# Second attention's last step moved into the closing stage, and the opening's joined weights scaled before a tile's norm

## The chip, the cores and the metric

The kernel runs on one core of one Trainium2 chip. The metric is device time in microseconds (us) of one execution. The kernel before took 2147.05 us (median of three runs, 2145.66 to 2149.94).

## The reference

Two transformer layers with adaptive layer norm run one after the other on x of shape (2, 1024, 512). For each layer, six modulation vectors come from a small projection of a conditioning input:

```python
mod = (silu(c) @ wmod)                              # sa, ca, ga, sb, cb, gb
h = layernorm(x) * (1 + ca) + sa
x = x + ga * attention(h, ...)
h = layernorm(x) * (1 + cb) + sb
x = x + gb * ffn(h, ...)
```

Layer 0's attention has 32 heads with a latent key and value of width 32, RMS norms and rotary parts of width 64. Its feed-forward adds experts weighted by a sparsemax. Layer 1's attention has 32 heads of width 16 that share one key and one value:

```python
scores = einsum('bqhd,bkd->bhqk', q, k) * scale     # causal
probs = softmax(scores);  out = einsum('bhqk,bkd->bqhd', probs, v) @ wo
```

Its feed-forward is a product with a weight to which a masked, Fourier-transformed low-rank update is added ("w_feed1").

## The kernel before

The kernel is one sequence of stages, and each engine's order of work is written out by hand. Each stage is a block: within it every engine runs its own list, held together by semaphores, and at its end all engines meet before the next block begins. The stages are: constants; opening; attention of layer 0; middle (closing of layer 0, queries and keys of layer 1); attention of layer 1; closing. Between some blocks stands `clear` (L63), a block of its own in which the sync engine sets every semaphore of a group to zero, one instruction for each, while the other engines wait.

**The end of layer 1's attention** (`attention1`, L1578). Its work goes in 16 steps (`STEPS1`) of 4 heads, and every step has two halves of 512 query columns. The TensorE adds up four heads' values and sums of probabilities in the PSUM tile `op`, and ScalarE copies each half out into `u_sb` (`copy_out`, L1670). The sync queue then runs `results(t)` (L1615): four transfers move the heads' rows to `att_t`, one writes the sums to DRAM (L1620), and, when that has landed, one reads them back spread over 128 partitions as `den` (L1622). VectorE takes the reciprocal (L1723). The sync queue runs `reciprocals(t)` (L1624): one transfer writes them to DRAM (L1626), and four read them back, each row broadcast over 16 partitions, as `spread` (L1632). GpSimd multiplies the step's 64 rows of `att_t` by `spread` (L1698). For steps 0 to 14 this runs beside the next step's scores. For step 15 nothing else is left. After it come the end of the block, a `clear` of the stage's 26 semaphores (24 in `ATT1`, L1099, and the two `q_in`), and the closing block.

**The closing stage** (`closing`, L1865). It handles 16 tiles of 128 rows (`ALL`), of which the first 8 belong to the first batch entry. Step 15 writes rows of the second entry alone, which tile 8 is the first to read. For tile n: ScalarE rounds the attention output to `a_hi` (`outcome`, L1947), GpSimd forms the remainder `a_lo` (L1962), the TensorE multiplies both with the output weights in 12 matmuls (`project`: L1896, L1897, and L1900 for `a_lo`), VectorE gates it, adds the input tile `xt` and takes the norm's statistics (`first`, L1983 to L1991), ScalarE takes the root, VectorE normalises into `xn` (L1998), the TensorE transposes (L1907), ScalarE modulates and rounds (`modulate`, L1939, L1943), GpSimd forms the remainder `h_lo` (`normed`, L1967), the TensorE multiplies with the feed-forward weights (L1914, L1915, L1918), and VectorE finishes (`second`) with the result in `x2`, which the sync queue stores (L1886). The loop over slots on each engine places `project(slot)` beside `turn(slot - 2)` and `feed(slot - 4)` on the TensorE, and `outcome(slot + 1)` beside `normed(slot - 2)` on GpSimd. At the block's start the sync queue issues four loads of 1 MB each for `xt` (L1883).

**The opening** (`opening`, L110). A tile group g is four tiles of 128 rows. The TensorE multiplies per-head weights into a latent product (`lat`, L286) in two PSUM banks (`op_wps`). VectorE scales them out into `l_wq` (`scaled`, L544), and that frees the banks for the joined output weights (`joined`, L296), whose matmuls stand in the TensorE's list ahead of `products(4)` (L328). VectorE's list reads:

```python
                statistics(1)
                normalise(1)
                rms(0)
                scaled()
                statistics(2)
```

`rms(0)` copies the products out of PSUM (L505), waits for ScalarE's squares of them (L409, L410), and goes on with the RMS norm and rotary parts (L508 to L528). ScalarE modulates the next group (L402) after those squares.

Of the kernel before, what the change touches and what calls it, by code (L numbers as in the profile page):

```python
# [13 lines left out]
ALU = mybir.AluOpType  # L14
# [95 lines left out]
def opening(nc, k, t, x_in, scratch, s):  # L110
# [3 lines left out]
    with ExitStack() as ctx:  # L114
# [69 lines left out]
        with nc.Block() as block:  # L184
# [272 lines left out]
            def _(dve):  # L457
# [82 lines left out]

                def scaled():
                    dve.wait_ge(s["lat_psum"], 1)
                    for c in range(2):
                        nc.vector.tensor_scalar(wq[:, 4 * c:4 * c + 4, 0, :], bank("lat", c)[:].rearrange("p (g n) -> p g n", n=P),  # L544
                                                lnw[:, 0:1], SCALE0, ALU.mult, ALU.mult).then_inc(s["lat_done"], 1)
# [29 lines left out]
                statistics(1)  # L575
                normalise(1)
                rms(0)
                scaled()
                statistics(2)
# [997 lines left out]

def attention1(nc, k, q_dram, sums, recips, stale, queries_in, next_loads, closed):  # L1578

    with ExitStack() as ctx:  # L1580
        sb = lambda n, sh, d=F32: ctx.enter_context(nc.sbuf_tensor("as_" + n, sh, d))
        ps = lambda n, sh: ctx.enter_context(nc.psum_tensor("as_" + n, sh, F32))
        s = {**semaphores(ctx, nc, "t1_", ATT1), **queries_in}
# [4 lines left out]
        u_sb = sb("u_sb", [P, 2, S])  # L1588
        den, rec, spread = sb("den", [P, 2, G * S // P]), sb("rec", [P, 2, G * S // P]), sb("spread", [P, S])
        scp = [ps(f"scp{i}", [P, HALF]) for i in range(BANKS1)]  # L1590
# [12 lines left out]
        with nc.Block() as block:  # L1603
            @block.sync
            def _(sp):
                def move(t):
                    move_queries(sp, q[t % SLOTS1], q_dram, t, q_in[t % SLOTS1])

                def maxima_row(t):
                    sp.wait_ge(s["mrow_done"], t + 1)  # L1610
                    for jj in range(2):
                        sp.dma_start(words(q[t % SLOTS1][RG * jj + MAXROW:RG * jj + MAXROW + 1, :, :]),
                                     words(mrow[jj * G * TILES // 2:(jj + 1) * G * TILES // 2, t % 2, :])).then_inc(m_in[t % SLOTS1], 16)

                def results(t):  # L1615
                    sp.wait_ge(s["u_copied"], 2 * t + 2)
                    for j in range(G):
                        r = RG * (t % 2) + HD * j
                        sp.dma_start(k.att_t[r:r + HD, t // NG, t % NG // 2, :], u_sb[2 * HD * j:2 * HD * j + HD, t % 2, :]).then_inc(s["u_moved"], 16)
                    sp.dma_start(sums[t], u_sb[HD:P:2 * HD, t % 2, :]).then_inc(s["sum_out"], 16)  # L1620
                    sp.wait_ge(s["sum_out"], 16 * (t + 1))
                    sp.dma_start(den[:, t % 2, :], sums[t].rearrange("j (c e) -> (j c) e", e=G * S // P)).then_inc(s["sum_in"], 16)  # L1622

                def reciprocals(t):  # L1624
                    sp.wait_ge(s["recip_done"], t + 1)
                    sp.dma_start(recips[t].rearrange("j (c e) -> (j c) e", e=G * S // P), rec[:, t % 2, :]).then_inc(s["recip_out"], 16)  # L1626
                    sp.wait_ge(s["recip_out"], 16 * (t + 1))
                    if t >= 2:
                        sp.wait_ge(s["att_done"], t - 1)
                    for j in range(G):  # L1630
                        r = RG * (t % 2) + HD * j
                        sp.dma_start(spread[r:r + HD, :], recips[t][j:j + 1, :].to_broadcast([HD, S])).then_inc(s["recip_in"], 16)  # L1632
                move(2)
                next_loads(sp)
                maxima_row(0)
                for t in range(STEPS1):
                    if t >= 1:
                        if t + 3 < STEPS1:
                            sp.wait_ge(s["sc_ready"], SCORES1 * t)
                            move(t + 3)  # L1640
                        results(t - 1)
                    elif t + 3 < STEPS1:
                        move(t + 3)
                    if t + 1 < STEPS1:
                        maxima_row(t + 1)
                    if t >= 1:
                        reciprocals(t - 1)
                results(STEPS1 - 1)
                reciprocals(STEPS1 - 1)

            @block.scalar
            def _(act):
# [12 lines left out]
                def copy_out(t, hf):  # L1665
                    act.wait_ge(s["pv_done"], t * QUADS + (12 if hf else 4))
                    if t >= 2:
                        act.wait_ge(s["u_moved"], 16 * G * (t - 1))
                        act.wait_ge(s["sum_out"], 16 * (t - 1))
                    nc.scalar.activation(u_sb[:, t % 2, HALF * hf:HALF * (hf + 1)], op[:], ACT.Copy).then_inc(s["u_copied"], 1)  # L1670

# [17 lines left out]
            @block.gpsimd  # L1689
            def _(pool):  # L1690
                for sem in stale.values():
                    pool.sem_clear(sem)
                def normalise(t):
                    h = RG * (t % 2)
                    a = k.att_t[h:h + RG, t // NG, t % NG // 2, :]
                    pool.wait_ge(s["u_moved"], 16 * G * (t + 1))
                    pool.wait_ge(s["recip_in"], 16 * G * (t + 1))
                    nc.gpsimd.tensor_tensor(a, a, spread[h:h + RG, :], ALU.mult).then_inc(s["att_done"], 1)  # L1698
                for t in range(STEPS1):
                    normalise(t)  # L1700

            @block.vector
            def _(dve):
# [14 lines left out]

                def reciprocal(t):
                    dve.wait_ge(s["sum_in"], 16 * (t + 1))  # L1720
                    if t >= 2:
                        dve.wait_ge(s["recip_out"], 16 * (t - 1))
                    nc.vector.reciprocal(rec[:, t % 2, :], den[:, t % 2, :]).then_inc(s["recip_done"], 1)  # L1723

                def split_weights(i):
# [11 lines left out]
                for g in range(QSETS):  # L1737
                    for u in range(LEAD + MQUAD * g, min(LEAD + MQUAD * (g + 1), MSTEP * STEPS1)):
                        maximum(u)
                    if g % QUADS == 8 and g >= QUADS:  # L1740
                        reciprocal(g // QUADS - 1)
                    if g % QUADS == 2 and g // QUADS in range(2, 2 + 2 * C):
                        split_weights(g // QUADS - 2)
                reciprocal(STEPS1 - 1)
                dve.wait_ge(s["w_lo"], 2 * C)

            @block.tensor
            def _(pe):
# [95 lines left out]
                for g in (QSETS - 2, QSETS - 1):  # L1844
                    values(*divmod(g, QUADS))
        clear(nc, s)

# [16 lines left out]

def closing(nc, k, x_in, x_out_dram, s):  # L1865

    with ExitStack() as ctx:
        sb = lambda n, sh, d=F32: ctx.enter_context(nc.sbuf_tensor("fg_" + n, sh, d))  # L1870
        ps = lambda n, sh: ctx.enter_context(nc.psum_tensor("fg_" + n, sh, F32))
        x_in_sem, x_out = [s[f"x_in{i}"] for i in range(GH)], [s[f"x_out{i}"] for i in range(XSLOTS)]
        xt, x1, xn, x2 = sb("xt", [P, GH, TH, D]), sb("x1", [P, XSLOTS, D]), sb("xn", [P, 2, D]), sb("x2", [P, XSLOTS, D])
        h_t, h_hi, h_lo = sb("h_t", [P, 2, C, P]), sb("h_hi", [P, 2, C, P], F32R), sb("h_lo", [P, 2, C, P], F32R)
# [4 lines left out]
        with nc.Block() as block:  # L1879
            @block.sync  # L1880
            def _(sp):
                for g in range(GH):
                    sp.dma_start(xt[:, g], x_in[HALF * g:HALF * (g + 1), :].rearrange("(n p) d -> p n d", p=P)).then_inc(x_in_sem[g], 16)  # L1883
                for n in range(ALL):
                    sp.wait_ge(s["x2_done"], n + 1)
# [43 lines left out]
            def _(act):  # L1929
# [14 lines left out]

                def outcome(n):
                    past(act, s["y_psum"], n + 1 - ASLOTS)
                    nc.scalar.activation(a_hi[:, n % ASLOTS], att(n), ACT.Copy).then_inc(s["ahi_done"], 1)  # L1947
# [10 lines left out]
            def _(pool):  # L1958
# [9 lines left out]
                outcome(0)  # L1968
                for slot in range(LAST):
                    if slot + 1 < ALL:  # L1970
                        outcome(slot + 1)
# [4 lines left out]
            def _(dve):  # L1976
# [24 lines left out]
                def second(n):  # L2001
# [56 lines left out]
def layers(nc, k, t, x_in, out, scratch):  # L2058
    with ExitStack() as ctx:
# [9 lines left out]
        with ExitStack() as inner:  # L2069
# [21 lines left out]
        closed = semaphores(ctx, nc, "fg_", CLOSE)  # L2091
        attention1(nc, k, queries, dram("sums1", (STEPS1, G, S)), dram("recips1", (STEPS1, G, S)), between, queries_in,
                   lambda sp: closing_loads(sp, k, t, scratch["w_feed1"], closed), closed)
        closing(nc, k, scratch["x_mid"], out, closed)
        clear(nc, closed)

# [88 lines left out]
```

## Time and profile before

| what | value |
|---|---|
| median of three runs | 2147.05 us |
| the profiled execution, its own time | 2148.23 us |
| its span in the trace | 2146.4 us |
| TensorE busy | 1964.6 us (92%) |
| VectorE, ScalarE, GpSimd busy | 1174.6, 903.1, 524.5 us |
| granted TensorE clock, mean | 0.946 of full |

The span is the stretch that the profiler's records cover. The execution's own time is 1.8 us longer. A busy time says how long an engine had an instruction in flight; idle time is put down to whatever released the engine afterwards. The stages stand in the trace as: opening to about 123 us, attention of layer 0 to the middle stage (ends about 1460 us), attention of layer 1 from about 1463 to 2035 us, closing from 2036 us on.

### The profile page before, as it was taken

The numbers are of one execution on the slowest core, as the hardware profiler recorded it, in microseconds if no ns is written. First come the engines' busy times: TensorE is split into PE (matmuls) and PEld (weight loads), VectorE is DVE, ScalarE is ACT, GpSimd is POOL, SyncE is SP. The second block draws the span as 40 slices with busy tenths as digits, with TensorE's granted clock in tenths as the row PEclk, the third lists the DMA queues.
The fourth block names the chain that finished last, engine by engine and source line by source line (L and its number), as shares of the span: only waits on it lengthen the run. The fifth ranks groups of instructions, "written<-read, shape, count | busy, mean of one in ns | idle before, by whom it ended". The sixth has DMA issues, their size and how long they took to land. (4 is left out here: it accounts for less than half of the span.)

```text
span 2146.4 us, 34674 instructions
## 1 busy us (share of the span) xinstructions
PE 1964.6 (92%) x12824; PEld 1177.3 (55%) x12824; DVE 1174.6 (55%) x2557; ACT 903.1 (42%) x1909; POOL 524.5 (24%) x408
## 2 busy tenths in 40 slices
PE   4859999999999999999986899997999999999698
PEld 4635666666666666666643454553444444444377
DVE  3536655555555555555401454446676767765078
ACT  2513344444444444444440122221666656656444
POOL 0014245555434444555330000000000000000143
PEclk8969999999999999999998999996999999999799
DMA  9742233222333233322236221144132222210121
GB/s 308 272 143 60 61 80 81 62 58 58 76 81 80 71 80 80 80 60 57 66 93 198 69 69 48 51 111 134 22 53 42 38 52 39 42 37 19 33 88 59
DMA packets 113594, 172.21 MB, mean 80 GB/s; under 512 B 26186, under 2 KB 46826, under 8 KB 113298
## 3 DMA queue, kind: packets, MB, share of 16 engines
q1 hardware_dynamic: 112402, 169.75, 29.8%
q8 instruction: 101, 1.65, 0.3%
q14 instruction: 67, 0.55, 0.1%
q10 hardware_dynamic: 1024, 0.26, 0.1%
HBM read 84.32 MB, written 29.38 MB: 53 GB/s over the span
## 5 line engine op out<-in xcount | busy, mean ns | idle before, releaser
L890 ACT ACTIVATE at_prob<-at_scp 128x512 f32<-128x512 f32 (+1 forms) x608 | 349.8, 576 | 515.4 <-PE at_scp L993 514.4
L1663 ACT ACTIVATE as_prob<-as_scp 128x512 f32<-128x512 f32 (+2 forms) x640 | 308.7, 564 | 197.5 <-PE as_scp L1773 148.2
L925 DVE CUSTOM_DVE_ANT_0 at_junk<-at_mxp,causal 128x128 f32<-128x128 f32 (+3 forms) x512 | 243.5, 488 | 190.5 <-PE at_mxp L1004 185.7
L1713 DVE TENSOR_REDUCE as_mxd<-as_mxp 128x2 f32<-128x256 f32 (+3 forms) x256 | 202.6, 820 | 98.3 <-PE as_mxp L1792 96.1
L920 DVE TENSOR_REDUCE at_mxf<-at_mxp 128x1 f32<-128x512 f32 x256 | 176.0, 688 | 143.4 <-PE at_mxp L1004 139.6
L1698 POOL TENSOR_TENSOR l_att_t<-l_att_t,as_spread 64x1024 f32<-64x1024 f32 x16 | 37.9, 2368 | 860.3 <-DMA as_spread<-l_recips 860.3
L820 POOL TENSOR_TENSOR at_pre<-at_prob 128x512 f32<-128x512 f32 x64 | 80.1, 1281 | 410.6 <-ACT at_prob L890 410.6
L1711 DVE TENSOR_REDUCE as_mxf<-as_mxp 128x2 f32<-128x1024 f32 x128 | 151.0, 1221 | 52.8 <-PE as_mxp L1787 52.6
L820 POOL TENSOR_TENSOR at_pre<-at_pre,at_prob 128x512 f32<-128x512 f32 x128 | 160.5, 1284 | 3.6 <-ACT at_prob L890 1.2
L1817 PE MATMUL as_op<-as_prob,l_vn 128*32 128x512 f32 (+3 forms) x1536 | 158.1, 533 | 0.3 <-ACT as_u_sb L1670 0.3
L989 PE MATMUL at_scp<-hd_early_q,l_khi 97*128 97x512 f32 (+1 forms) x304 | 138.3, 455 | 11.3 <-DMA hd_late_q<-at_slo 8.2
L1026 PE MATMUL at_op<-at_prob,l_cn 128*32 128x512 f32 (+3 forms) x1536 | 144.4, 493 | 4.0 <-ACT at_u_sb L861 4.0
L989 PE MATMUL at_scp<-at_qhi,l_khi 97*128 97x512 f32 (+1 forms) x304 | 138.7, 456 | 0.8 <-ACT at_prob L890 0.5
L1004 PE MATMUL at_mxp<-l_khi,hd_early_q 96*128 96x512 f32 (+2 forms) x384 | 126.2, 383 | 10.5 <-DMA hd_early_q<-at_shi 9.3
L1004 PE MATMUL at_mxp<-l_khi,at_qhi 96*128 96x512 f32 (+2 forms) x384 | 122.5, 367 | 0.5 <-DVE at_tm L950 0.2
L992 PE MATMUL at_scp<-hd_late_q,l_khi 96*128 96x512 f32 (+1 forms) x304 | 118.0, 388 | 0.0
L993 PE MATMUL at_scp<-hd_early_q,l_klo 96*128 96x512 f32 (+1 forms) x304 | 117.7, 387 | 0.0
L992 PE MATMUL at_scp<-at_qlo,l_khi 96*128 96x512 f32 (+1 forms) x304 | 116.8, 384 | 0.0
L993 PE MATMUL at_scp<-at_qhi,l_klo 96*128 96x512 f32 (+1 forms) x304 | 116.3, 383 | 0.0
L1787 PE MATMUL as_mxp<-l_keys,hd_early_q 48*128 48x512 f32 (+2 forms) x384 | 97.7, 488 | 19.2 <-DVE as_mxf L1711 7.3
L1770 PE MATMUL as_scp<-as_q,l_keys 49*128 49x512 f32 (+2 forms) x320 | 105.3, 444 | 7.4 <-ACT as_prob L1663 5.9
L1770 PE MATMUL as_scp<-hd_early_q,l_keys 49*128 49x512 f32 (+2 forms) x320 | 103.6, 445 | 5.7 <-ACT as_prob L1663 4.3
(250 smaller groups left out, 3494.4 us busy)
## 6 DMA issues: line engine op xcount, KB each, us to landing
hd_late_q<-at_slo SPq DMA_DIRECT2D x96, 128.0 KB, 2.4
at_qhi<-at_shi SPq DMA_DIRECT2D x96, 128.0 KB, 2.5
at_qlo<-at_slo SPq DMA_DIRECT2D x96, 128.0 KB, 2.4
hd_early_q<-at_shi SPq DMA_DIRECT2D x84, 128.0 KB, 2.4
at_spread<-l_recips SPq DMA_DIRECT2D x64, 128.0 KB, 2.7
l_o<-at_u_sb SPq DMA_DIRECT2D x16, 512.0 KB, 3.4
hd_early<-in_wmod SPq DMA_DIRECT2D x7, 1024.0 KB, 6.8
hd_late<-l_o SPq DMA_DIRECT2D x12, 512.0 KB, 4.1
```

What stands on the lines that cost most here:

```text
L820: nc.gpsimd.tensor_tensor(pre[:, j, :], other, prob[:, (x + j) % RING0, :], ALU.add).then_inc(s["pre_done"], 1)
L890: nc.scalar.activation(prob[:, x % RING0, c0:HALF], scp[x % BANKS0][:, c0:HALF], ACT.Exp).then_inc(s["exp_done"], 1)
L920: nc.vector.reduce_max(mxf[:, j, qt - 4:qt - 3], tile[:], AX_X).then_inc(s["mx_done"], 1)
L925: nc.vector.tensor_tensor_reduce(out=junk[:, u % 2, 0:w], in0=tile[:, 0:w], in1=k.causal[:, HALF - w:HALF], scale=1.0, scalar=LOWEST, op0= ...
L989: nc.tensor.matmul(out, k.khi[0:KR + 1, b, ks], q_cols(qhi[t % 2][0:KR + 1]), start=True, stop=False)
L992: nc.tensor.matmul(out, k.khi[0:KR, b, ks], q_cols(qlo[t % 2][0:KR]), start=False, stop=False)
L993: nc.tensor.matmul(out, k.klo[0:KR, b, ks], q_cols(qhi[t % 2][0:KR]), start=False, stop=True).then_inc(s["sc_ready"], 1)
L1004: nc.tensor.matmul(bank("max", t, u)[:, 0:w], qhi[t % 2][0:KR, qt // 4, j, qt % 4 * P:(qt % 4 + 1) * P], k.khi[0:KR, t // NG, k0:k0 + w], ...
L1663: nc.scalar.activation(prob[:, x % RING1, cols], scp[x % BANKS1][:, cols], ACT.Exp).then_inc(s["exp_done"], 1)
L1713: nc.vector.reduce_max(mxd[:, t % 2, :, i, qt:qt + 1], tile[:, :, 0:(qt % 4 + 1) * P], AX_X).then_inc(s["mx_done"], 1)
L1770: mm = nc.tensor.matmul(out, k.keys[rows, t // NG, kt * P:(kt + 1) * P], queries, start=True, stop=not diagonal)
L1817: mm = nc.tensor.matmul(op[2 * HD * j:2 * HD * (j + 1), c0:HALF], k.vn[:, t // NG, kt, :], prob[:, (x + j % UNITS1_OF[n]) % RING1, p0:p0 + ...
```

## The change

The functions `results`, `reciprocal`, `reciprocals` and `normalise` become methods of a class `Outcomes`, with the same instructions, and are called from two stages. Steps 0 to 14 stay where they were. For step 15:

- The sync queue runs `results(15)` and `reciprocals(15)` in the closing block, after the first of the four `xt` loads and ahead of the other three.
- VectorE runs `reciprocal(15)` as its first instruction in the closing block.
- GpSimd runs `normalise(15)` in slot 3 of its closing list, between `normed(0)` and `outcome(4)`, with three waits on its own and the DMA's semaphores around it.
- ScalarE waits for `normalise(15)` before it rounds tile 8.
- The buffers `u_sb`, `den`, `rec` and `spread` live past the attention stage; in the closing stage `xn` and `x2` are laid over `k.late`, which held unsplit weights.
- The `clear` of 26 semaphores between the two blocks goes; the same semaphores are cleared in the last block, after the closing stage, together with the closing stage's 31.

In the opening, `scaled()` moves ahead of `rms(0)` in VectorE's list, with a wait for the small loads.

```diff
@@VectorE's functions in the opening
                 def scaled():
+                    dve.wait_ge(s["small_in"], 64)
                     dve.wait_ge(s["lat_psum"], 1)
...
                 normalise(1)
+                scaled()
                 rms(0)
-                scaled()
                 statistics(2)
@@
+class Outcomes:
+    def __init__(self, nc, k, s, sums, recips):
+        self.nc, self.k, self.s, self.sums, self.recips = nc, k, s, sums, recips
+
+    def results(self, sp, t):
+        k, s = self.k, self.s
+        sp.wait_ge(s["u_copied"], 2 * t + 2)
+        for j in range(G):
+            r = RG * (t % 2) + HD * j
+            sp.dma_start(k.att_t[r:r + HD, t // NG, t % NG // 2, :], k.u1[2 * HD * j:2 * HD * j + HD, t % 2, :]).then_inc(s["u_moved"], 16)
+        sp.dma_start(self.sums[t], k.u1[HD:P:2 * HD, t % 2, :]).then_inc(s["sum_out"], 16)
+        sp.wait_ge(s["sum_out"], 16 * (t + 1))
+        sp.dma_start(k.den1[:, t % 2, :], self.sums[t].rearrange("j (c e) -> (j c) e", e=G * S // P)).then_inc(s["sum_in"], 16)
+
+    def reciprocal(self, dve, t):
+        k, s = self.k, self.s
+        dve.wait_ge(s["sum_in"], 16 * (t + 1))
+        if t >= 2:
+            dve.wait_ge(s["recip_out"], 16 * (t - 1))
+        self.nc.vector.reciprocal(k.rec1[:, t % 2, :], k.den1[:, t % 2, :]).then_inc(s["recip_done"], 1)
+
+    def reciprocals(self, sp, t):
+        k, s = self.k, self.s
+        sp.wait_ge(s["recip_done"], t + 1)
+        sp.dma_start(self.recips[t].rearrange("j (c e) -> (j c) e", e=G * S // P), k.rec1[:, t % 2, :]).then_inc(s["recip_out"], 16)
+        sp.wait_ge(s["recip_out"], 16 * (t + 1))
+        if t >= 2:
+            sp.wait_ge(s["att_done"], t - 1)
+        for j in range(G):
+            r = RG * (t % 2) + HD * j
+            sp.dma_start(k.spread1[r:r + HD, :], self.recips[t][j:j + 1, :].to_broadcast([HD, S])).then_inc(s["recip_in"], 16)
+
+    def normalise(self, pool, t):
+        k, s = self.k, self.s
+        h = RG * (t % 2)
+        a = k.att_t[h:h + RG, t // NG, t % NG // 2, :]
+        pool.wait_ge(s["u_moved"], 16 * G * (t + 1))
+        pool.wait_ge(s["recip_in"], 16 * G * (t + 1))
+        self.nc.gpsimd.tensor_tensor(a, a, k.spread1[h:h + RG, :], ALU.mult).then_inc(s["att_done"], 1)
@@attention1
                     if t >= 1:
-                        reciprocals(t - 1)
-                results(STEPS1 - 1)
-                reciprocals(STEPS1 - 1)
+                        outcomes.reciprocals(sp, t - 1)
...
-                for t in range(STEPS1):
-                    normalise(t)
+                for t in range(STEPS1 - 1):
+                    outcomes.normalise(pool, t)
...
-                reciprocal(STEPS1 - 1)
                 dve.wait_ge(s["w_lo"], 2 * C)
...
-        clear(nc, s)
@@closing
-        xt, x1, xn, x2 = sb("xt", [P, GH, TH, D]), sb("x1", [P, XSLOTS, D]), sb("xn", [P, 2, D]), sb("x2", [P, XSLOTS, D])
+        xt, x1, xn, x2 = sb("xt", [P, GH, TH, D]), sb("x1", [P, XSLOTS, D]), *[k.late[:, lo:hi].rearrange("p (n d) -> p n d", d=D) for lo, hi in ((0, 2 * D), (2 * D, (2 + XSLOTS) * D))]
...
                     sp.dma_start(xt[:, g], x_in[HALF * g:HALF * (g + 1), :].rearrange("(n p) d -> p n d", p=P)).then_inc(x_in_sem[g], 16)
+                    if g == 0:
+                        outcomes.results(sp, STEPS1 - 1)
+                        outcomes.reciprocals(sp, STEPS1 - 1)
...
                 def outcome(n):
+                    if n == TILES:
+                        act.wait_ge(outcomes.s["att_done"], STEPS1)
                     past(act, s["y_psum"], n + 1 - ASLOTS)
...
                 for slot in range(LAST):
+                    if slot == 3:
+                        pool.wait_ge(s["alo_done"], slot + 1)
+                        pool.wait_ge(s["lo_done"], 1)
+                        outcomes.normalise(pool, STEPS1 - 1)
+                        pool.wait_ge(outcomes.s["att_done"], STEPS1)
                     if slot + 1 < ALL:
                         outcome(slot + 1)
...
+                outcomes.reciprocal(dve, STEPS1 - 1)
                 for slot in range(LAST + 1):
                     if slot < ALL:
                         first(slot)
@@layers
+        attended1 = {**semaphores(ctx, nc, "t1_", ATT1), **queries_in}
...
-        clear(nc, closed)
+        clear(nc, closed, attended1)
```

## Rows read from the trace of the kernel before

**Rows 1.** Timeline: start, length, engine, line, tiles, [idle before <- releaser]; between stages.

```profile
2018.97 0.60 ACT L1670 ACTIVATE as_u_sb<-as_op 128x512 f32<-128x512 f32 x1 [2.00 <-PE as_op L1817]
2019.60 2.42 SPq L1619 DMA_DIRECT2D l_att_t<-as_u_sb  x4
2023.93 0.34 SPq L1622 DMA_DIRECT2D as_den<-l_sums  x1
2025.65 0.35 DVE L1723 RECIPROCAL as_rec<-as_den 128x32 f32<-128x32 f32 x1 [27.18 <-DMA as_den<-l_sums]
2031.08 2.34 POOL L1698 TENSOR_TENSOR l_att_t<-l_att_t,as_spread 64x1024 f32<-64x1024 f32 x1 [25.21 <-DMA as_spread<-l_recips]
2035.94 2.63 SPq L1883 DMA_DIRECT2D fg_xt<-scratch_x_mid  x4
2036.64 0.80 PE L1896 MATMUL fg_yps<-l_wo_hi,fg_a_hi 128*128 128x512 f32 x1 [17.73 <-ACT fg_a_hi L1947]
```

**Rows 2.** The same view, opening.

```profile
16.14 0.43 SPq L220 DMA_DIRECT2D op_lnw<-in_q_ln  x1
42.40 1.15 DVE L505 COPY op_raw<-op_aps 128x448 f32<-128x448 f32 x2
45.59 2.89 ACT L402 ACTIVATE op_h_t<-op_hps,mod 128x128 f32<-128x128 f32 x8
48.13 1.40 DVE L544 TENSOR_SCALAR l_wq<-op_wps,op_lnw 128x512 f32<-128x512 f32 x2
49.02 3.25 PE L296 MATMUL op_wps<-hd_late,op_wv 128*32 128x512 f32 x16 [6.18 <-DVE l_wq L544]
52.19 1.78 PE L328 MATMUL op_aps<-op_wa,op_h_t 128*128 128x224 f32 x8
55.85 1.06 PE L296 MATMUL op_wps<-op_ring,op_wv 128*32 128x512 f32 x8
68.17 2.77 PE L328 MATMUL op_aps<-op_wa,op_h_t 128*128 128x224 f32 x8 [2.84 <-ACT op_h_t L402]
73.51 1.07 PE L296 MATMUL op_wps<-hd_late,op_wv 128*32 128x512 f32 x8
```

**Rows 3.** The same view, closing stage: its first tiles.

```profile
2041.83 0.39 PE L1896 MATMUL fg_yps<-l_wo_hi,fg_a_hi 128*128 128x512 f32 x1
2042.03 0.69 DVE L1983 TENSOR_TENSOR fg_x<-fg_yps,l_gates 128x512 f32<-128x512 f32 x1 [16.03 <-PE fg_yps L1900]
2049.16 0.68 DVE L1983 TENSOR_TENSOR fg_x<-fg_yps,l_gates 128x512 f32<-128x512 f32 x1
2054.18 0.61 ACT L1947 ACTIVATE fg_a_hi<-l_att_t 128x512 fp32r<-128x512 f32 x1
2054.94 0.47 PE L1896 MATMUL fg_yps<-l_wo_hi,fg_a_hi 128*128 128x512 f32 x1 [2.40 <-ACT fg_a_hi L1947]
2055.59 1.28 POOL L1962 TENSOR_TENSOR fg_a_lo<-l_att_t,fg_a_hi 128x512 fp32r<-128x512 f32 x1
2058.12 1.39 PE L1900 MATMUL fg_yps<-l_wo_hi,fg_a_lo 128*128 128x512 f32 x4
```

**Rows 4.** The same view: end of the constants block, start of the opening.

```profile
3.11 0.29 DVE L2034 CAST after_r<-co_after 128x256 fp32r<-128x256 f32 x1 [0.20 <-POOL co_after L2053]
4.23 0.86 SPq L210 DMA_DIRECT2D op_cin<-in_c  x2
```

**Rows 5.** Timeline, and the waits of the sync queue: the end.

```profile
2141.87 0.33 SPq L1886 DMA_DIRECT2D out<-fg_x  x1
SPq L1888 <- DMA out<-fg_x: 1.7, 1, 1.7
```

**Rows 6.** DMAs: time to landing of L1883; KB and median us to landing.

```profile
DMA to landing us min/median/max: 5.7/9.1/12.3
...
op_lnw<-in_q_ln SPq DMA_DIRECT2D x1, 0.5 KB, 12.3
```

**Rows 7.** Windows: length, busy of each engine, granted clock, DMA share, GB/s.

```profile
2054.00:2058.00 4.00, 3.06 (x8) 2.48 (x9) 2.69 (x5) 3.46 (x9) 2.79 (x3) 0.67 0.00 0
```

More of the change, by code:

```diff
@@ L1575, in max_banks, with attention1 @@
     return {what: (i % MXBANKS, order[i - MXBANKS] if i >= MXBANKS else None) for i, what in enumerate(order)}
-def attention1(nc, k, q_dram, sums, recips, stale, queries_in, next_loads, closed):
+class Outcomes:
[33 more added lines that the diff above has]
+        self.nc.gpsimd.tensor_tensor(a, a, k.spread1[h:h + RG, :], ALU.mult).then_inc(s["att_done"], 1)
+def attention1(nc, k, q_dram, s, outcomes, stale, next_loads, closed):
     with ExitStack() as ctx:
@@ L1582, in attention1 @@
         ps = lambda n, sh: ctx.enter_context(nc.psum_tensor("as_" + n, sh, F32))
-        s = {**semaphores(ctx, nc, "t1_", ATT1), **queries_in}
         q = first_queries1(k) + [sb(f"q{i}", [P, PAIRS, S], F32R) for i in range(2, SLOTS1)]
@@ L1587, in attention1 @@
         mrow = sb("mrow", [G * TILES, 2, P], F32R)
-        u_sb = sb("u_sb", [P, 2, S])
-        den, rec, spread = sb("den", [P, 2, G * S // P]), sb("rec", [P, 2, G * S // P]), sb("spread", [P, S])
         scp = [ps(f"scp{i}", [P, HALF]) for i in range(BANKS1)]
@@ L1613, in maxima_row @@
                                      words(mrow[jj * G * TILES // 2:(jj + 1) * G * TILES // 2, t % 2, :])).then_inc(m_in[t % SLOTS1], 16)
[L1615 to L1632, printed above, removed]
                 move(2)
@@ L1640, in _ @@
                             move(t + 3)
-                        results(t - 1)
+                        outcomes.results(sp, t - 1)
                     elif t + 3 < STEPS1:
@@ L1669, in copy_out @@
                         act.wait_ge(s["sum_out"], 16 * (t - 1))
-                    nc.scalar.activation(u_sb[:, t % 2, HALF * hf:HALF * (hf + 1)], op[:], ACT.Copy).then_inc(s["u_copied"], 1)
+                    nc.scalar.activation(k.u1[:, t % 2, HALF * hf:HALF * (hf + 1)], op[:], ACT.Copy).then_inc(s["u_copied"], 1)
                 def maxima_out(t):
@@ L1692, in _ @@
                     pool.sem_clear(sem)
[L1693 to L1698, printed above, removed]
-                for t in range(STEPS1):
-                    normalise(t)
+                for t in range(STEPS1 - 1):
+                    outcomes.normalise(pool, t)
             @block.vector
@@ L1717, in maximum @@
                         nc.vector.tensor_tensor(late, late, mxf[:, t % 2], ALU.max).then_inc(s["mx_joined"], 1)
[L1719 to L1723, printed above, removed]
                 def split_weights(i):
@@ L1740, in _ @@
                     if g % QUADS == 8 and g >= QUADS:
-                        reciprocal(g // QUADS - 1)
+                        outcomes.reciprocal(dve, g // QUADS - 1)
                     if g % QUADS == 2 and g // QUADS in range(2, 2 + 2 * C):
                         split_weights(g // QUADS - 2)
-                reciprocal(STEPS1 - 1)
                 dve.wait_ge(s["w_lo"], 2 * C)
@@ L1862, in closing_loads, with closing @@
             sp.dma_start(k.gates1[:, b, a, :], k.gate_rows[1][b][a:a + 1, :].to_broadcast([P, D])).then_inc(s["gates_in"], 16)
-def closing(nc, k, x_in, x_out_dram, s):
+def closing(nc, k, x_in, x_out_dram, s, outcomes):
     with ExitStack() as ctx:
@@ L2091, in layers @@
         closed = semaphores(ctx, nc, "fg_", CLOSE)
-        attention1(nc, k, queries, dram("sums1", (STEPS1, G, S)), dram("recips1", (STEPS1, G, S)), between, queries_in,
+        k.u1, k.spread1 = sb("u1", [P, 2, S]), sb("spread1", [P, S])
+        k.den1, k.rec1 = sb("den1", [P, 2, G * S // P]), sb("rec1", [P, 2, G * S // P])
+        attended1 = {**semaphores(ctx, nc, "t1_", ATT1), **queries_in}
+        outcomes = Outcomes(nc, k, attended1, dram("sums1", (STEPS1, G, S)), dram("recips1", (STEPS1, G, S)))
+        attention1(nc, k, queries, attended1, outcomes, between,
                    lambda sp: closing_loads(sp, k, t, scratch["w_feed1"], closed), closed)
-        closing(nc, k, scratch["x_mid"], out, closed)
-        clear(nc, closed)
+        closing(nc, k, scratch["x_mid"], out, closed, outcomes)
+        clear(nc, closed, attended1)
 def build(nc, t, out, scratch):
```

## The prediction

> **What bounds the kernel now.** I read the timeline from one stage to the next, then the chain of waits. The TensorE is busy in nearly all of the span, so what can be won lies in the stretches where it stands. Two are touched by the change. The long one lies between the stages [rows 1]: ScalarE's last copy ends at 2019.57, and the TensorE starts again at 2036.64 after 17.73 us idle. Read the rows in order and a serial chain appears: four moves and the sums out, the sums back (the reciprocal starts 6.05 us after the first issue), the reciprocals out and in, and GpSimd's product (31.08 to 33.42). Nothing else runs. Then 2.52 us go by until the closing block's first load. The second stretch is in the opening [rows 2]: the weights' matmuls (L296) begin at 49.02 after 6.18 us idle, released by VectorE's L544.
>
> In the closing stage the start is not bound by the TensorE [rows 3]. VectorE's first product starts at 2042.03, and the TensorE's fifth tile only at 2054.94, after 2.40 us idle. VectorE and ScalarE take turns there. From that tile on, the chain of waits runs along the TensorE alone to the last tile. So two things decide: when VectorE starts its first tile, and whether the fifth tile's remainder product (L1900 at 2058.12) is late.
>
> **Start of the closing block.** The block can start once ScalarE's copy is out. Cost of a block's end: the constants stage's last instruction ends at 3.40 and the opening's first issue is at 4.23 [rows 4], 0.83 us for two meetings of the engines and five clears. Between attention and closing, 2.52 us hold two meetings and 26 clears [rows 1]. The 21 further clears take 1.69 us, 0.080 us each, and a meeting about 0.2 us. The end of the kernel agrees: the last store is issued at 2141.87, its data is there 1.7 us after the issue is out (2143.90) [rows 5], and the remaining 2.5 us of the span divided by 31 clears is 0.081. I take 0.35 us for one meeting with the start of a block: closing starts at 2019.92 instead of 2035.94.
>
> **VectorE's first tile.** Before, it starts 6.1 us after the block's start, when the TensorE has its first tile. This tile ran at the low clock: L1896 of the first tile at 2036.64, of the second at 2041.83, 5.2 us [rows 1, 3]. Now VectorE waits first for `reciprocal(15)`, behind which its whole list is queued. The sync queue issues the first `xt` load (about 0.5 us of the 2.63 us for four), then the chain: from the moves' issue to the reciprocal 6.05 us, and the reciprocal 0.35 us [rows 1]. If the transfers don't meet, that is 0.5 + 6.05 + 0.35 = 6.9 us after the start. But the 1 MB load stands ahead in the same queue. It lands 5.7 us after its issue, at best [rows 6], and a small transfer waits for what was issued before it: `op_lnw`, 0.5 KB, landed 12.3 us after its issue behind the opening's megabytes [rows 6]. So the sums reach DRAM not before 0 + 5.7 plus about 0.8 us for the four moves, 6.5 us, then 1.72 us from the issue of their reading back (2023.93) to the reciprocal (2025.65), then 0.35: about 8.6 us. Ends: 6.9 and 9.5 us (slower issues beside a full queue). I take 8.6, since the queued row is the nearer case. VectorE's first tile then starts at 2028.5, which is 13.5 us earlier.
>
> The Trainium skill ("DMA: Bandwidth & Descriptors", Queues, rings and completion order) says that on each DMA engine the descriptors of one issuing engine's ring are consumed in the order in which they were put in, though completions of different transfers have no such order. By it the small moves stand behind the load, as the row suggests; without it the block would win 1.7 us more.
>
> **From VectorE's first tile to the fifth tile.** Before, 12.15 us pass between them (2042.03 to ScalarE's rounding of tile 4 at 2054.18) [rows 3]; the instructions stay. The clock changes. The TensorE finishes tiles 0 and 1 about 6 us after the block's start, then has nothing until ScalarE rounds tile 2, another 6 us on. 2.40 us idle were enough for the clock to fall: 0.67 granted between 2054 and 2058 [rows 7]. So I expect tile 2 at 1.2 GHz, 5.2 us instead of 2.9. VectorE wants it 7.1 us after its first tile (2049.16 against 2042.03) [rows 3], and it would come about 8.2 us after: 1.0 us lost. Ends: 0 and 1.5.
>
> The Trainium skill ("TensorE: Matmul & The Clock Gate", What's actually happening) calls the throttled clock the default, which activity releases. The clock row above agrees; where the change leaves the TensorE waiting, this rule speaks against it.
>
> **GpSimd's product in slot 3.** Before, the remainder of tile 4 (L1962) starts at 2055.59 and takes 1.28 us; the TensorE takes it up at 2058.12, so the slack is 1.25 us [rows 3]. `normalise(15)` adds 2.34 us [rows 1] and about 0.1 for its waits: 2.44 - 1.25 = 1.2 us of waiting, less a little that the eight matmuls at low clock cost anyway. I take 1.1. Its own inputs are there: the broadcast reciprocals land some 14 us after the block's start, and slot 3 comes about 21 us after it. Behind it in GpSimd's list are the remainders of tile 5 and later, two of 1.3 us a tile against a tile of nearly 6 us on the TensorE, so that the lateness is gone within two tiles. The other three `xt` loads go out about 12 us after the block's start and the first is needed about 12 us later: hidden, with a landing of at most 12.3 us for three in a row [rows 6] and about 6 for the first. If that cover failed, it would cost the difference. ScalarE's wait before tile 8 is over long before. The overlaid buffers and the class cost nothing: same instructions.
>
> **The clears.** Those of the 26 semaphores leave the seam (counted in the 2.52 us), and come back at the end, where only the sync engine works: 26 x 0.081 = +2.1 us. Ends: 1.7 and 2.5.
>
> Sum of the closing part: -13.5 + 1.0 + 1.1 + 2.1 = -9.3 us; with the fifth tile's matmuls at the full clock part of the time, the low-clock stretch of before saves 0.3: -9.0 with a rounding. Ends: -7.4 and -12.4.
>
> **The opening** [rows 2]. VectorE is at `rms(0)` at 42.40. With L544 first (1.40 us) the first bank is free at 43.1 and the matmuls L296 run from about 43.2 instead of 49.0. They then end by 45 to 46.5. Next comes L328 for tile 4, which needs ScalarE's modulation (L402), and that stands behind the squares, which wait for L505, now 1.4 us later. ScalarE's 2.89 us for two tiles begin at 47.0 instead of 45.59, so tile 4 is ready at 48.45. Before, L328 began at 52.19: 3.74 us won, and that limit is a new wait. The idle time before it, 2 to 3.3 us, costs clock. The stage shows it: after 2.84 us idle eight L328 take 2.77 us (at 68.17) against 1.78 (at 52.19), and from there to the next L296 it is 73.51 - 68.17 = 5.34 us against 55.85 - 52.19 = 3.66, 1.7 us more. So -3.74 + 1.7 = -2.1 us (ends -1.5 and -3.7). The rest of the opening is a chain through TensorE, ScalarE and VectorE whose loads are issued when a slot is freed, so it moves up with it. The added wait costs nothing: the last small load, issued at 16.14, lands 12.3 us later, 14 us before VectorE asks [rows 2, 6]. `statistics(2)` starts when it did.
>
> **Total**: -9.0 - 2.1 = -11.1 us. The profiled execution's own time is 2148.23 us (span 2146.4 and 1.8 around it), which gives 2137.1. It lies 1.2 us above the median of the runs, 2147.05, and from this one: 2136.0 us.
>
> **The rivals.**
> - The small moves pass the load, and the TensorE keeps its clock in both places (20%). For it: the TensorE is busy until 2019 and starts again 1.6 us later. Against: the clock and landing rows [rows 6, 7]. Then -15.1 (VectorE's first tile at 2026.9) + 1.1 + 2.1 in the closing part and -3.7 in the opening: -15.6, 2131.4 us.
> - The waits turn into longer stretches at 1.2 GHz (20%). For it: the TensorE now has three idle stretches of 2 us or more in the closing stage's start, where half the clock costs 2.3 us a tile. Another 2.5 us in the closing part, and 1 in the opening: -7.6, 2139.5 us.
> - Slower than before: the closing stage's steady run falls to 1.2 GHz (3%). It began after 17.7 us of rest in which the TensorE did nothing; that rest goes. At half clock a tile of 5.9 us takes twice as long, so the gain is eaten after 11.1 / 5.9, about two tiles of 16, and with four such tiles the kernel is 12 us slower: 2159 us. Against it: outside of gaps the clock has not been seen to fall for long.
> - The change does not do what it says (2%): the end of the block is held by something else than ScalarE's copy, for one a late instruction of the sync queue, and closing begins no earlier. Then the clears only change places, and the opening's 2.1 us remain: 2145 us.
>
> **How the numbers follow.** The forecast has 55%. It and the first two rivals give faster. What a measurement of this kernel can tell from no change is about 0.2%, 4 us. Faster 95%, within it 2%, slower 3%. The range goes from just under the first rival to the second: 2131 to 2140 us.
>
> **What the changed kernel's profile would show.** The last copy (L1670) followed by the rounding of tile 0 within 0.5 us; the reciprocal of step 15 about 8.3 us after the block's start, and VectorE's first gating right behind it, not behind the TensorE; a granted clock of half near tile 2; GpSimd's 64x1024 product between two products of 128x512, and the TensorE idle about 1 us before tile 4's L1900, released by GpSimd; about 4.6 us between the last landing and the end of the span. In the opening: L296 right after L544 at about 43, then L328 at 48.4, released by L402. I am wrong in size if the reciprocal comes 6.5 us after the block's start, and wrong in kind if the last tiles' L1918 keep their distance from the span's beginning.

## The result, and the profile after

The changed kernel takes 2138.27 us (median of 6 runs, 2135.04 to 2140.92) against 2146.95 us (6 runs, 2143.1 to 2149.94): ratio 0.9962, 95% interval 0.9952 to 0.9973, which is 5.8 to 10.3 us less. The forecast was 2136.0 us, and 11.1 us less. The profiled execution took 2136.10 us with a span of 2134.3 us, 12.1 us under the span of before; it lies 2.2 us under its median, and the one of before 1.3 us over its own.

Timeline of the changed kernel between the stages (start, length, engine, line, tiles, [idle before <- releaser]); it answers to [rows 1] and [rows 3]:

```profile
2017.39 0.60 ACT L1691 ACTIVATE l_u<-as_op 128x512 f32<-128x512 f32 x1 [2.00 <-PE as_op L1825]
2018.25 0.38 SPq L1890 DMA_DIRECT2D fg_xt<-scratch_x_mid  x1
2018.68 2.41 SPq L1590 DMA_DIRECT2D l_att_t<-l_u  x4
2025.22 0.34 SPq L1593 DMA_DIRECT2D l_den<-l_sums  x1
2026.78 0.35 DVE L1600 RECIPROCAL l_rec<-l_den 128x32 f32<-128x32 f32 x1 [29.88 <-DMA l_den<-l_sums]
2027.05 0.63 DVE L2000 TENSOR_TENSOR fg_x<-fg_yps,l_gates 128x512 f32<-128x512 f32 x1
...
2030.35 0.76 PE L1906 MATMUL fg_yps<-l_wo_hi,fg_a_hi 128*128 128x512 f32 x1 [5.66 <-ACT fg_a_hi L1959]
...
2034.71 0.69 DVE L2000 TENSOR_TENSOR fg_x<-fg_yps,l_gates 128x512 f32<-128x512 f32 x1 [0.52 <-PE fg_yps L1910]
```

The closing block starts 0.26 us after the last copy's end (2017.99 to 2018.25); before, this took 16.4 us. VectorE's first instruction is the reciprocal, 8.5 us after the block's start, and its first tile follows at once. By then the TensorE has finished tiles 0 and 1; it stands idle for 5.66 us until tile 2. Tile 2 begins at the low clock (0.73 granted between 2028 and 2032) and comes 0.52 us late for VectorE.

The same view, tile 4 of the closing stage:

```profile
2039.37 0.61 ACT L1959 ACTIVATE fg_a_hi<-l_att_t 128x512 fp32r<-128x512 f32 x1
2040.95 2.38 POOL L1619 TENSOR_TENSOR l_att_t<-l_att_t,l_spread 64x1024 f32<-64x1024 f32 x1
2041.01 2.61 DVE L2015 TENSOR_SCALAR hd_late<-fg_x,fg_mv,fg_sd 128x512 f32<-128x512 f32 x1
...
2043.41 1.32 POOL L1974 TENSOR_TENSOR fg_a_lo<-l_att_t,fg_a_hi 128x512 fp32r<-128x512 f32 x1
...
2044.79 1.19 PE L1910 MATMUL fg_yps<-l_wo_hi,fg_a_lo 128*128 128x512 f32 x4 [2.58 <-POOL fg_a_lo L1974]
```

GpSimd's 64x1024 product stands between tile 3's and tile 4's work, and the TensorE waits 2.58 us for the remainder of tile 4. In [rows 3] it did not wait there.

The opening (the same view), with the lines of [rows 2]:

```profile
42.87 1.41 DVE L545 TENSOR_SCALAR l_wq<-op_wps,op_lnw 128x512 f32<-128x512 f32 x2
43.76 1.92 PE L296 MATMUL op_wps<-hd_late,op_wv 128*32 128x512 f32 x16 [0.35 <-DVE l_wq L545]
...
47.38 2.88 ACT L402 ACTIVATE op_h_t<-op_hps,mod 128x128 f32<-128x128 f32 x8
...
48.92 2.27 PE L328 MATMUL op_aps<-op_wa,op_h_t 128*128 128x224 f32 x8 [3.24 <-ACT op_h_t L402]
```

The wait for L544 (L545 in the changed kernel) went from 6.18 to 0.35 us, and a new wait of 3.24 us for ScalarE stands behind it.

I cut every trace at the same events. The table gives the pieces in us: "opening" runs from VectorE's reciprocal of group 1 (L468) to attention 0's first matmul, "middle" from there to the end of the last copy (L1670 before), "start" from there to VectorE's first tile, "to tile 4" from there to ScalarE's rounding of it, "remainder" from there to tile 4's L1900 (before), "run" from there to VectorE's last instruction, "end" to the end of the span.

| kernel | opening | middle | start | to tile 4 | remainder | run | end |
|---|---|---|---|---|---|---|---|
| before | 82.93 | 1896.29 | 22.46 | 12.15 | 3.94 | 83.72 | 4.56 |
| changed | 80.97 | 1896.20 | 9.06 | 12.32 | 5.42 | 83.53 | 5.98 |
| e1 opening alone | 82.78 | 1895.80 | 22.44 | 12.16 | 3.92 | 83.73 | 4.62 |
| e2 closing alone | 82.85 | 1892.33 | 9.26 | 12.28 | 5.42 | 83.53 | 5.97 |
| e7 chain back | 81.43 | 1895.73 | 19.66 | 12.16 | 4.15 | 83.41 | 5.98 |
| e3 reciprocal later | 82.09 | 1896.35 | 4.02 | 14.63 | 5.41 | 85.28 | 6.02 |
| e4 product in slot 5 | 80.88 | 1892.40 | 9.20 | 12.30 | 2.76 | 83.52 | 5.99 |
| e5 load split | 83.51 | 1895.52 | 6.94 | 12.11 | 5.42 | 85.22 | 6.00 |
| e6 clears inside | 83.86 | 1895.34 | 9.19 | 12.36 | 5.42 | 83.53 | 4.58 |
| e8 the three | 83.99 | 1895.06 | 4.01 | 14.82 | 2.76 | 83.53 | 4.57 |
| e9 as e8, opening undone | 82.99 | 1892.23 | 4.01 | 14.64 | 2.75 | 83.53 | 4.60 |
| e10 as e8, scaled earlier | 79.31 | 1892.76 | 4.02 | 14.56 | 2.75 | 83.53 | 4.59 |
| e11 as e8, load split | 83.82 | 1892.54 | 4.02 | 13.65 | 4.10 | 83.59 | 4.63 |
| e12 e10 and e11 | 80.73 | 1895.79 | 4.06 | 13.94 | 4.26 | 83.42 | 4.60 |

Between kernels with the same closing stage, the closing columns repeat within some 0.3 us; the exceptions are the runs of e3 and e5, 1.7 us longer, which e3 below takes up. The opening and the middle do not repeat. The middle, which no kernel changes, falls into two groups: 1892.2 to 1892.8 us in five traces (e2, e4, e9, e10, e11) and 1895.1 to 1896.4 us in the other nine. The split is there before attention 1: its first load of queries is issued 1335.5 to 1336.0 us after attention 0's first matmul in the five, and 1338.6 to 1339.8 us in the nine. What decides it stays open. A difference of 3.5 us between two spans, or between two medians of six runs, can come from there.

### The profile page after: what moved, and what is told of

It is laid out like the page before. It is cut to its first block and busy times, and to the rows that moved or that the text cites. A ratio compares the mean times of both kernels' runs of the same rounds, so it can differ in the third digit from the quotient of the medians.

```text
span 2134.3 us, 34666 instructions
## 1 busy us (share of the span) xinstructions
PE 1965.5 (92%) x12824; PEld 1179.6 (55%) x12824; DVE 1178.3 (55%) x2557; ACT 902.4 (42%) x1909; POOL 524.8 (25%) x408
## 5 line engine op out<-in xcount | busy, mean ns | idle before, releaser
L1619 POOL TENSOR_TENSOR l_att_t<-l_att_t,l_spread 64x1024 f32<-64x1024 f32 x16 | 37.9, 2366 | 834.4 <-DMA l_spread<-l_recips 834.3
L990 PE MATMUL at_scp<-hd_early_q,l_khi 97*128 97x512 f32 (+1 forms) x304 | 138.2, 455 | 11.1 <-DMA hd_late_q<-at_slo 8.0
L1005 PE MATMUL at_mxp<-l_khi,hd_early_q 96*128 96x512 f32 (+2 forms) x384 | 126.2, 383 | 10.5 <-DMA hd_early_q<-at_shi 9.3
```

What stands on the lines that cost most here:

```text
L990: nc.tensor.matmul(out, k.khi[0:KR + 1, b, ks], q_cols(qhi[t % 2][0:KR + 1]), start=True, stop=False)
L1005: nc.tensor.matmul(bank("max", t, u)[:, 0:w], qhi[t % 2][0:KR, qt // 4, j, qt % 4 * P:(qt % 4 + 1) * P], k.khi[0:KR, t // NG, k0:k0 + w], ...
```

## The experiments

**e1, the opening's move alone** (on the kernel before):

```diff
                 def scaled():
+                    dve.wait_ge(s["small_in"], 64)
...
+                scaled()
                 rms(0)
-                scaled()
```

> The kernel before with the opening's move alone (scaled ahead of the first RMS norm). Theory: the new limit is ScalarE's modulation, with the TensorE at the low clock behind it, so from the rounding of group 1's norm (L468) to the first projection of attention 0 the stage takes 2.0 us less, and the kernel 2.0 us less than before. Rival: the opening's gain is given back before the stage's end by the loads (0 us). Rival: the clock does not matter, 3.7 us.

2146.52 us against 2146.39 for the kernel before, measured beside it; ratio 1.0002 (0.9992 to 1.0011), from 1.7 us less to 2.4 more. The opening took 82.78 us, against 82.93 before. The theory's 2.0 us are not there.

**e2, the closing part alone** (on the changed kernel):

```diff
-                scaled()
                 rms(0)
+                scaled()
```

> The changed kernel with the opening's move undone: the closing part alone. Theory: the parts add, 10.5 us less than before in the trace (span), of it 13.4 from the last copy of attention 1 to VectorE's first tile, given back 1.5 at tile 4 and 1.4 at the end. Rival: the changed kernel's true gain is only its median difference of 8.7 us, so that this one shows about 6.7 in its trace as well.

2136.85 against 2146.39, ratio 0.9953 (0.9939 to 0.9968): 6.9 to 13.1 us less. Its columns from "start" to "end" add up to 10.4 us less than before, as in the changed kernel (10.5). Its whole span is 16.5 us shorter, but 4 us of this are the middle, which it does not touch, and 2 lie ahead of the opening's cut. The closing part is the whole of the gain that the runs can show.

**e7, the chain back in the attention stage:**

```diff
                         outcomes.reciprocals(sp, t - 1)
+                outcomes.results(sp, STEPS1 - 1)
+                outcomes.reciprocals(sp, STEPS1 - 1)
...
-                for t in range(STEPS1 - 1):
+                for t in range(STEPS1):
                     outcomes.normalise(pool, t)
...
+                outcomes.reciprocal(dve, STEPS1 - 1)
                 dve.wait_ge(s["w_lo"], 2 * C)
```

and the same calls taken out of the closing stage.

> The changed kernel with step 15's sums, reciprocals and product back in the attention stage, in its buffers of now; the clears stay at the end. Theory: of the 2.5 us between GpSimd's product and the closing block's first load only one meeting of the engines is left (0.4 us), the end is 1.4 us longer: 2.7 us less than before with the opening's 2.0. The serial chain is thus worth 9 us or more. Rival: most of the closing gain comes from the clear that is gone; then this is within 3 us of the changed kernel.

2145.14 against 2146.39, ratio 0.9995 (0.9984 to 1.0006), which is less than the 2.7 us expected; the opening's 2.0 us were part of that sum. The block starts 14.09 us after the copy's end instead of 16.37, so the clear and one meeting of the engines were worth 2.3 us there, and the end takes 1.4 us longer. Of the 13.4 us won at the start, 10.6 are the chain's (19.66 to 9.06). The rival, that the clear was most of the gain, falls.

**e3, the reciprocal after VectorE's first tile:**

```diff
-                outcomes.reciprocal(dve, STEPS1 - 1)
                 for slot in range(LAST + 1):
                     if slot < ALL:
                         first(slot)
+                    if slot == 0:
+                        outcomes.reciprocal(dve, STEPS1 - 1)
```

> The changed kernel with VectorE's reciprocal of step 15 after its first tile's gating and statistics instead of ahead of them. Theory: VectorE's head waits 4 us for the queue's round trips; now its first product starts when the TensorE has tile 0, 3.6 us after the block's start instead of 8.8, the addition waits for the 1 MB load (5.3 us), and the gain after one tile is 3.2 us against the changed kernel. Rival: the load of the input lands no earlier than the sums come back, gain under 1 us.

2135.05, ratio 0.9947 (0.9933 to 0.9961). VectorE's first product starts 3.76 us after the block's start. Its addition then waits for the 1 MB load until 6.95 us, longer than the 5.3 expected, and tile 4 comes 2.7 us earlier than in the changed kernel (18.65 against 21.38 after the copy). A low-clock stretch in the run (0.60 granted between 2044 and 2048) took 1.8 us of it in this trace, so that from the copy's end it is only 1.0 us shorter than the changed kernel's (115.4 against 116.3), and not 3.2. The medians differ by 3.2 us, but their intervals overlap. The stretch stands behind GpSimd's product: the TensorE waits 2.59 us for tile 4's remainder and then gets the low clock. e5 has the same wait (2.60 us, then 0.70 granted between 2044 and 2048, run 85.22); the changed kernel, e2 and e6 have it (2.58 us) and lose nothing behind it (run 83.53). In none of the five traces from e8 on, whose product is in slot 5, does the run exceed 83.6.

**e4, GpSimd's product in slot 5:**

```diff
-                    if slot == 3:
+                    if slot == 5:
                         pool.wait_ge(s["alo_done"], slot + 1)
-                        pool.wait_ge(s["lo_done"], 1)
+                        pool.wait_ge(s["lo_done"], slot - 2)
```

> The changed kernel with GpSimd's product of step 15 in slot 5 instead of slot 3. Theory: the TensorE's 2.58 us of waiting before tile 4's remainder product (L1910) is GpSimd's doing, and later there is slack: 2.4 us less than the changed kernel. Rival: the lateness only moves to tile 6, 0.5 us or less.

2133.86 against 2145.62, ratio 0.9941 (0.9929 to 0.9954). The timeline of e4, tile 4's remainder and where the product went:

```profile
2035.94 1.29 POOL L1974 TENSOR_TENSOR fg_a_lo<-l_att_t,fg_a_hi 128x512 fp32r<-128x512 f32 x1
...
2037.29 1.19 PE L1910 MATMUL fg_yps<-l_wo_hi,fg_a_lo 128*128 128x512 f32 x4
...
2044.77 2.41 POOL L1619 TENSOR_TENSOR l_att_t<-l_att_t,l_spread 64x1024 f32<-64x1024 f32 x1
```

The "remainder" is 2.76 us instead of 5.42, and the run stays at 83.52: the 2.7 us are gone, not moved. (The ratio's interval overlaps that of the changed kernel, so it is the trace that shows this.)

**e5, the first load split** around the small moves:

```diff
-                    sp.dma_start(xt[:, g], x_in[HALF * g:HALF * (g + 1), :] ...).then_inc(x_in_sem[g], 16)
+                x(0, 0, 1)
+                outcomes.results(sp, STEPS1 - 1)
+                x(0, 1, TH)
+                outcomes.reciprocals(sp, STEPS1 - 1)
...
```

`x(g, lo, hi)` loads tiles lo to hi of group g; tile 1's addition waits for the second part.

> The changed kernel, with only a quarter of the first input load (256 KB) ahead of the small moves and the other 768 KB behind them. Theory: the sums wait in the queue behind 1 MB; with 256 KB ahead VectorE's reciprocal starts 7.1 us after the block's start instead of 8.5, and the kernel gains 1.4 us. Rival: the small moves take their time by themselves (issue and landing), the reciprocal stays at 8.5.

2134.91, ratio 0.9946 (0.9934 to 0.9958). The timeline of e5:

```profile
2017.67 0.34 SPq L1890 DMA_DIRECT2D fg_xt<-scratch_x_mid  x1
2018.06 2.41 SPq L1590 DMA_DIRECT2D l_att_t<-l_u  x4
2020.52 0.53 SPq L1591 DMA_DIRECT2D l_sums<-l_u  x1
2022.38 0.34 SPq L1593 DMA_DIRECT2D l_den<-l_sums  x1
...
2024.08 0.35 DVE L1600 RECIPROCAL l_rec<-l_den 128x32 f32<-128x32 f32 x1 [27.51 <-DMA l_den<-l_sums]
```

From the sums' issue to the reading back 1.86 us pass; with 1 MB ahead it was 4.08 (2021.14, in the chain of waits below, to 2025.22). In the kernel before, with no load ahead, it was 1.87 us (2022.06 to 2023.93), so 256 KB cost these moves nothing. The reciprocal comes 6.4 us after the block's start, 2.1 us earlier, more than the 1.4 expected. The small moves do stand behind the 1 MB load. In this trace the low-clock stretch takes most of it back.

**e6, the 26 clears inside the closing block:**

```diff
+                    if n == ALL - 4:
+                        for sem in outcomes.s.values():
+                            sp.sem_clear(sem)
...
-        clear(nc, closed, attended1)
+        clear(nc, closed)
```

> The changed kernel with the attention stage's 26 semaphores cleared by the sync queue inside the closing block, after the 13th store, while it would wait. Theory: from the last store's issue to the end of the span 4.5 us as in the kernel before, instead of 6.0: 1.4 us less. Rival: the time at the end is not the clears', no change.

2133.13, ratio 0.9934 (0.992 to 0.9949). The end is 4.58 us instead of 5.98, as before the change. The median lies 5.1 us below the changed kernel's, further than 1.4 us, and the interval just misses that of the changed kernel (0.9952 to 0.9973). From the copy's end the trace shows 1.2 us and nothing more; where the rest comes from is not shown.

**e8, the three together:**

> The changed kernel with the reciprocal after the first tile, GpSimd's product in slot 5, and the 26 clears inside the closing block. Theory: the three add, 3.2 + 2.4 + 1.4 = 7.0 us less than the changed kernel, about 19 us less than before in the trace. Rival: with VectorE's start earlier the TensorE's first product of the steady run is bound by something else and half of it is lost, 3.5 us.

2128.56 against 2145.62, ratio 0.9917 (0.9904 to 0.993), 15 to 21 us less than before. From the copy's end the trace has 6.6 us less than the changed kernel's (109.7 against 116.3) of the 7.0 expected.

**e9, e8 with the opening's move undone:**

> e8 with the opening's move undone. Theory now: the move wins 2 to 3 us up to the third block of joined weights (L296), but each idle stretch behind ScalarE in the opening is followed by a stretch at 1.2 GHz whose length varies from execution to execution (8 to 11 us from tile group 2's wait to the next weights), so that on the average 0.5 us are left: e9 within 1.5 us of e8 in the median. Rival: the opening's 2.0 us of the first trace are real, e9 is 2 us slower than e8.

2126.56 against 2144.34, ratio 0.9921 (0.9905 to 0.9936), beside e8's 0.9917: no difference to be seen, within some 3 us. With e1 this says that the opening's move is worth less than its 2.0 us in the trace promised, and perhaps nothing.

**e10, scaled ahead of the norm of group 1**, on e8:

```diff
+                scaled()
                 normalise(1)
-                scaled()
                 rms(0)
```

> e8 with the latent weights scaled ahead of the norm of group 1 (normalise), where VectorE stands idle waiting for ScalarE's root, so that nothing of the first RMS norm is delayed. Theory: tile 4's L328 comes 1.4 us earlier behind the norm than in e8; in the median 0 to 1.4 us less than e8, since the clock gives and takes. Rival: VectorE's wait for the latent product delays the norm, e10 slower than e8.

2124.85 against 2144.34, ratio 0.991 (0.9894 to 0.9927): the fastest, 16 to 23 us under before. The opening takes 79.31 us, and 80.73 in e12. In both, L328 of tile 4 waits 2.44 us instead of 3.24 and starts 6.8 us after the cut instead of 8.1. The medians of e8 and e10 are not far enough apart to tell them.

**e11, e8 with the load split** (a semaphore of its own for the first quarter):

> e8 with the first input load split: a quarter ahead of the small moves, the rest behind. In e8 VectorE's first addition waits for the 1 MB load until 7.1 us after the block's start. Theory: the quarter lands at about 4.5 us, the addition starts then and the tile after it 2.2 us earlier than in e8. Rival: then the reciprocal, whose sums come back at 6.4 us, or the second addition, whose input is in the rest, holds VectorE; gain under 1 us.

2127.86, ratio 0.992 (0.9906 to 0.9934). The first addition starts at 4.49 us instead of 7.13, but the second waits 1.89 us for the rest of the load, and tile 4's remainder is as late as in e8 (21.8 against 21.6 us after the copy). The rival holds.

**e12, both:**

> e10 and e11 together. Theory: the sum of both, 1.5 to 3.5 us less than e8, some 20 us less than before. Rival: no more than e8.

2126.88, ratio 0.9915 (0.9901 to 0.9929): no more than e8 or e10.

## Why the prediction was right, point by point

- **Start of the block and VectorE's first tile: -13.5 expected, -13.4 measured** (22.46 to 9.06). The meeting of the engines with the start of the block is 0.26 us (0.35 assumed). The reciprocal came 8.5 us after the start (8.3 expected; 6.5 would have been the first rival's), and the load ahead in the queue was the reason: e5. The chain of waits of the changed kernel shows it as one piece of transfer:

```profile
2021.14 4.06 DMA l_sums<-l_u
2025.22 1.54 DMA l_den<-l_sums
```

The load landed 6.3 us after its issue, at 2024.6, and the sums after it, just before 2025.22. The sentence of the Trainium skill ("DMA: Bandwidth & Descriptors", Queues, rings and completion order) on the order in one ring agrees with this trace. That strict order and not a shared bandwidth held the moves is not shown: no run separates the two. The load is slower too when small moves follow it: 6.3 us to land in the changed kernel and 6.9 in e3, against 5.7 for the first load in [rows 6].
- **Tile 2 at the low clock: +1.0 expected, +0.2 measured.** The mechanism is there, 5.66 us idle and 0.52 us of waiting. But the clock came back within tile 2, after 2033, so the product held the TensorE for 4.2 us (2030.35 to 2034.51) and not 5.2. The term was too large.
- **GpSimd in slot 3: +1.1 expected, +1.5 measured, and in truth 2.7.** I compared with tile 4 at the low clock, as it ran before. In the changed kernel its eight matmuls run at the full clock, so the TensorE arrives earlier and waits the longer: e4 wins 2.66 us. The product also takes VectorE with it. L2015, 0.55 us at the tiles around it, takes 2.61 us while GpSimd's runs. In e4 it is an addition (L2004, 0.69 us at the tile before) that takes 2.55 us beside the product, and there nothing is lost by it.
- **The clears at the end: +2.1 expected, +1.4 measured** (e6, e7). 26 clears cost 0.054 us each there. Between the stages they and one meeting cost 2.28 us (e7), so about 0.08 for one if a meeting is 0.2. Why the same instruction costs less at the end stays open; dividing the old end by its 31 clears probably counted other things with them.
- **Sum of the closing part: -9.0 expected, -10.5 in the trace, -10 (6.9 to 13.1 less) in e2's runs.** The recorded sum has a slip. It goes from -9.3 to -9.0 for a low-clock stretch that would save 0.3 us, but a saving makes it -9.6. Without the slip the closing part would have been nearer to the -10.5 us of the trace, and the whole forecast, 11.7 us less, farther from the 8.7 us of the runs.
- **The opening: -2.1 expected; -2.0 in the first trace, none in the runs.** This term was wrong, and that the first trace gave it was luck. In the three traces without the move the opening takes 82.85 to 82.99 us; in the nine with it (e10 and e12 place it elsewhere), from 80.88 to 83.99, mean 82.6. The first steps came as said: the wait for VectorE went, and L328 of tile 4 starts 8.10 us after the cut instead of 11.84, the 3.74 us of the forecast. But the gain is lost on the way. The third block of joined weights (55.85 in [rows 2]) starts 13.3 to 14.7 us after the cut instead of 15.5 to 16.9, on the mean 2.7 us earlier; the weights behind the next wait (73.51 in [rows 2]) 1.2 us earlier; attention 0 0.3 us earlier. What I had put down as a fixed price of 1.7 us is a scatter, and it recurs behind each later wait for ScalarE. The timeline shows it at the same eight matmuls after the same idle time. In e2:

```profile
67.44 1.78 PE L328 MATMUL op_aps<-op_wa,op_h_t 128*128 128x224 f32 x8 [2.84 <-ACT op_h_t L402]
```

The same line of the timeline in e8:

```profile
65.80 3.35 PE L328 MATMUL op_aps<-op_wa,op_h_t 128*128 128x224 f32 x8 [2.84 <-ACT op_h_t L402]
```

1.78 in e2, 2.77 in [rows 2], 3.35 us in e8: all, part and none of it at the full clock. The granted clock agrees: between 66 and 70 us it was 1.00 in e2 and 0.50 in e8, and in the kernel before 0.85, then 0.72 to 74. With the move the stage has three such waits for ScalarE (3.24, 2.84 and 2.82 us) and one of 2.53 us for VectorE, and in some executions it gives back what one edit wins.
- **The total.** The trace's pieces make -10.5 and about 0 for the opening; the runs say -8.7, between -5.8 and -10.3. The forecast's 11.1 was too high by the opening's term, and the closing term, too small by 1.5, hid part of it. That the total came as near as 2.4 us is in part luck. That the runs of this kernel lie near 2 us above the pieces' sum, while e2's do not, I cannot explain beyond the scatter of the middle. The rival of a slower steady run fell: 1.00 granted from 2052 to 2124. So did the one in which the closing block starts no earlier (it starts 0.26 us after the copy). The rival of longer stretches at 1.2 GHz did not come in the changed kernel's closing part, but e3 and e5 show that it can: 1.7 us there.

## What to carry to other kernels

A serial chain at the end of a stage is worth moving into the next when only a late tile needs its result, but its waits must not stand at the head of an engine that every tile needs: here that cost 2.7 us of 13, and GpSimd's slot another 2.7. Price an added instruction against the clock that the engine will run at after the change. Judge a change of 2 us by the cut pieces of several traces, not by the span of one.

## What the runs showed of the hardware that was not expected

- VectorE's tensor_scalar of 128x512 took 2.61 us beside a 2.38 us GpSimd product (changed kernel) and 0.55 us without it; an addition of the same size 2.55 us beside a 2.41 us product (e4) and 0.69 us without it.
- After an idle time of the same length (2.84 us) the TensorE ran the next eight matmuls in 1.78 (e2), 2.77 (before) or 3.35 us (e8).
- A semaphore's clear: about 0.08 us between two stages (e7), 0.054 at the end (changed kernel and e6).
- 16 KB issued behind 1 MB and four moves of 64 KB: 4.06 us until the sync queue went on; behind 256 KB and the moves 1.86 (e5), behind the moves alone 1.87 (before).
